# Half-precision products for the second experts' down projection, and GpSimd's stores without a turn marker

## The chip, the core and the metric

The kernel runs on one core of a Trainium2 chip. Its time is the device time of one execution in microseconds; smaller is better. The core's engines run their own instruction streams and wait for each other on semaphores: PE (TensorE, with PEld for its weight loads), DVE (VectorE), ACT (ScalarE), POOL (GpSimd) and SP (SyncE, which here only issues DMAs).

## The reference, cut to what matters

Two transformer layers of a gated cross-attention kind act on 64 x 64 tokens of width 128. Each layer adds an attention output and then the output of a mixture of eight experts, of which every token uses two. The last step, the one that the change touches most, is the second layer's mixture:

```python
perm = xf[rev]                               # 8192 slots, sorted by expert
chunks = perm.reshape(e, n * k // e, d)      # 8 experts x 1024 slots x 128
h = jax.nn.gelu(jnp.einsum('ecd,edf->ecf', chunks, w1), approximate=False)   # up, 128 -> 512
y = jnp.einsum('ecf,efd->ecd', h, w2).reshape(n * k, d)                      # down, 512 -> 128
y = y * sw[:, None]
out = jnp.zeros((n, d), dtype=x.dtype).at[rev].add(y)
```

The first layer's mixture has the same shape with relu and biases. All of it is in float32.

## The kernel before, in words

The work runs in four stages: first attention (0 to some 195 us of the trace), first experts (to 351), second attention (to 590), second experts (to the end). Each engine's order is written out by hand; the changes are in the two expert stages.

In an expert stage the 8192 slots are cut into tiles of 256: 32 tiles in four rounds of eight for the second experts; the first experts have four more tiles that serve two experts each. Rounds 2 and 3 are one loop body run twice, in a loop of the engine; rounds 1 and 4 are written out. Tile q goes through these steps:

- SP loads the tile's rows, gathered in DRAM, into `xin` (second experts: GpSimd gathers the first six tiles with indirect DMAs, line 592, and seven patches that SP stores back before it loads tile 6, lines 599 and 789).
- `gather` (PE, line 984): four half-precision transposes into PSUM; `parts` (DVE, line 1753) copies them to `xgT`.
- `up` (PE, line 996): twelve matmuls with 256 columns, in three half-precision products (high x high, high x low, low x high parts of the two factors).
- ACT's `step` (line 1281): gelu of 1024 columns from PSUM into `hid`, in float32.
- `down` (PE, line 1008): eight float32 matmuls with 128 columns, which the trace shows as sixteen rows.
- `result` (DVE, line 1777): two multiplications by the slots' weights into `yrow`.
- GpSimd's `step`: line 553, a multiplication of one element whose only use is its semaphore `turn`, and line 555, two indirect DMAs that store `yrow`. DVE waits for `turn` (line 1761) before it writes a `yrow` again.

PE's order in step q is gather of tile q+1, up of tile q, down of tile q-1. The expert of a tile is known only at run time. So for each `up` and each `down` PE's sequencer, the part of the engine that reads its instructions and hands the matmuls on, loads the expert's number (`expert`, line 1015) and computes weight addresses in its registers. These register instructions carry the line of the matmul that needs them, 803, since all matmuls go through `mm`.

Before the second experts, GpSimd scatters the tokens into DRAM (line 544) and SP loads `w2` after the last attention product (line 784).

Of the kernel before, what the change touches and what calls it, by code (L numbers as in the profile page):

```python
# [11 lines left out]
ALU = mybir.AluOpType  # L12
# [9 lines left out]
P = 128  # L22
# [48 lines left out]
def build(nc, A, out):  # L71

    ctx = ExitStack()
    with ctx:
# [69 lines left out]
        turn = sb("turn", [1, XS_LEAD])  # L144
# [29 lines left out]
        w2 = sb("w2", [P, E * FF])  # L174

# [56 lines left out]
        yrow = at(18.5, [XS_LEAD, 2, D])  # L232
        yc = at(44, [4, CT_TILES, TOPK, D])
# [29 lines left out]
        def banks(b, n):  # L263
# [31 lines left out]
        w2_in = sem("w2_in")  # L295
# [4 lines left out]
              (("xin", XS_LEAD), ("xT", 2), ("xT_sb", 2), ("up", 2), ("hid", 2), ("y", 2), ("yrow", 2), ("turn", 1),  # L300
# [13 lines left out]

        def turns(l, i, q):
            if l == 1 and isinstance(i, int) and i == 0:
                return (ROUNDS - (q >= MIXED)) * XS_LEAD + q + 1
            return l * TILES[0] + (i - 1) * XS_LEAD + q + 1
# [162 lines left out]
        def _(pool):  # L481
# [66 lines left out]
            def experts(l):  # L548

                def step(i, q):  # L550
                    pool.wait_ge(ff["yrow"][q % 2], i * (XS_LEAD // 2) + q // 2 + halves(l) + 1)

                    g.tensor_tensor(turn[:, q:q + 1], lane[0:1, :], lane[0:1, :], ALU.mult).then_inc(ff["turn"][0], 1)  # L553
                    for u in range(2):
                        g.indirect_dma_start(  # L555
                            ys[l], bass.IndirectOffsetOnAxis(xin[:, q, u, :].bitcast(U32)[:, D:D + 1], 0),
                            yrow[:, q, u, :], None).then_inc(ff["stored"][q], 16)

                expert_tiles(pool, l, step)
# [77 lines left out]
        def _(sp):  # L637
# [161 lines left out]
        def _(pe):  # L799
# [162 lines left out]
            def experts(l):  # L962
                f, m0 = ff, halves(l)
                pe.wait_ge(w1_lo[l], E)
                if l == 1:
                    pe.wait_ge(w2_in, 16)
# [33 lines left out]
                def down(i, q, es):  # L1000
                    v, m = q % 2, i * (XS_LEAD // 2) + q // 2 + m0
                    pe.wait_ge(f["hid"][v], m + 1)
# [13 lines left out]

                def round_(i, n, last):

                    first = isinstance(i, int) and i == 0
                    for q in range(n):  # L1020
                        late = first and (q == 0 or l == 1 and q == HEAD0 - 1)
                        if q < n - 1:
                            if not late:
                                gather(i, q + 1)
                        elif not last:
                            gather(i + 1, 0)
                        up(i, q, expert(i, q))
                        if q >= 1:
                            down(i, q - 1, expert(i, q - 1))
                        elif not first:  # L1030
                            down(i - 1, XS_LEAD - 1, expert(i - 1, XS_LEAD - 1))
                        if late:
                            gather(i, q + 1)
# [6 lines left out]
                if l == 0:  # L1040
                    pe.wait_ge(left, 1)
                    round_(ROUNDS, MIXED, True)
                    down(ROUNDS, MIXED - 1, expert(ROUNDS, MIXED - 1))
                else:
                    down(ROUNDS - 1, XS_LEAD - 1, expert(ROUNDS - 1, XS_LEAD - 1))
# [151 lines left out]
        def _(act):  # L1197
# [58 lines left out]
            def experts(l):  # L1256
# [6 lines left out]
                def step(i, q):  # L1263
                    v, m = q % 2, i * (XS_LEAD // 2) + q // 2 + m0
                    act.wait_ge(f["up"][v], m + 1)
                    wait(act, f["y"][v], m)
# [47 lines left out]
            for g in range(G0, G1):  # L1314
# [47 lines left out]
                for c in route_at("copy", g):  # L1362
                    route_copy(1, c)
            experts(1)
# [6 lines left out]
        def _(dve):  # L1371
# [374 lines left out]
            def experts(l):  # L1746
# [9 lines left out]
                def result(i, q):  # L1756
# [3 lines left out]
                    if l == 1 or not (isinstance(i, int) and i == 0):  # L1760
                        dve.wait_ge(f["turn"][0], turns(l, i, q))
# [13 lines left out]
                    for u in range(2):  # L1775
                        w = xin[:, q, u, :].bitcast(F32)[:, D + 1:D + 2]
                        ins = v_.tensor_scalar(yrow[:, q, u, :], y[:, u, :], w, None, ALU.mult)  # L1777
                    ins.then_inc(f["yrow"][v], 1)

                def round_(i, n, last):  # L1780
                    first = isinstance(i, int) and i == 0
                    for q in range(n):
# [4 lines left out]
                        if q >= 1:  # L1787
                            result(i, q - 1)
                        elif not first:
                            result(i - 1, XS_LEAD - 1)  # L1790
# [10 lines left out]
                else:  # L1801
                    result(ROUNDS - 1, XS_LEAD - 1)
# [95 lines left out]
            route_table(1)  # L1898
            experts(1)
# [50 lines left out]
```

## Time and profile before

| | us |
|---|---|
| median of three runs | 751.6 (748.81 to 752.73) |
| the profiled execution | 751.48 |
| its span, first to last instruction | 749.9 |
| PE busy | 543.9 (73%) |
| DVE busy | 416.3 (56%) |
| POOL busy | 330.3 (44%) |
| ACT busy | 231.4 (31%) |

What lies outside the span is 1.6 us. Busy shares are means over four stages with different limits, so the rows below are taken from the stages that the change touches.

### The profile page before, as it was taken

How to read it: one execution, taken by the hardware profiler on the slowest of the kernel's cores; microseconds unless marked ns; L12 is line 12 of the kernel's file. 1: busy time of each engine (PE TensorE's matmuls, PEld its weight loads, DVE VectorE, ACT ScalarE, POOL GpSimd, SP SyncE). 2: the span in 40 equal slices, each digit the busy share in tenths (PEclk: the TensorE clock that was granted, in tenths of full speed). 3: DMA queues.
4: the chain of work that ended last, by engine and by line, in shares of the span. 5: the costliest groups of instructions: out<-in, count | busy, mean ns of one | idle time of the engine just before them, and what ended most of it. 6: DMA issues, size and time to landing. Idle time of an engine off the chain costs nothing.

```text
span 749.9 us, 16972 instructions
## 1 busy us (share of the span) xinstructions
PE 543.9 (73%) x5388; PEld 427.4 (57%) x5389; DVE 416.3 (56%) x1474; ACT 231.4 (31%) x411; POOL 330.3 (44%) x412
## 2 busy tenths in 40 slices
PE   1687958515699999962798888696871487999950
PEld 1355646402289999952354567575650175989950
DVE  4785496997523333314896378878678421223315
ACT  0321011123044444432621365454542031323210
POOL 6202005777536666634500000071657676656650
PEclk9878685855799999996689999888665599999985
DMA  7911001123222222411763255453333123322219
GB/s 206 264 46 35 23 14 34 50 96 100 72 76 83 73 77 79 122 65 52 242 200 125 69 153 163 112 133 81 68 100 104 45 55 105 80 79 77 72 51 321
DMA packets 70254, 74.97 MB, mean 100 GB/s; under 512 B 12216, under 2 KB 58552, under 8 KB 70120
## 3 DMA queue, kind: packets, MB, share of 16 engines
q1 hardware_dynamic: 55240, 49.64, 24.1%
q0 software_dynamic: 9968, 21.88, 9.4%
q10 hardware_dynamic: 4976, 2.53, 1.2%
q8 instruction: 43, 0.70, 0.4%
q14 instruction: 27, 0.22, 0.1%
HBM read 45.62 MB, written 28.29 MB: 99 GB/s over the span
## 4 chain that ended last, share of the span: by engine, by line
PE 54%; DVE 20%; issue 8%; POOL 8%; DMA 6%; ACT 2%; SPq 1%; POOLq 0%; DVEq 0%; ACTq 0%
PE PS L803 49%; POOL xs L544 5%; DMA work<-ys 3%; DVE XN L1424 2%; PE PS L984 2%; DVE X L1381 2%; DVE work L1381 1%; DVE work L1865 1%; POOL work L592 1%; DVE rtmp L1381 1%; DVE stats L1386 1%; PE PS L1145 1%; POOL work L599 1%; PE PS L832 1%; DVE nwt L1381 1%
## 5 line engine op out<-in xcount | busy, mean ns | idle before, releaser
L544 POOL DMA_INDIRECT xs<-pack,adr_i x80 | 78.0, 975 | 188.8 <-ACT pack L1220 136.5
L555 POOL DMA_INDIRECT ys<-work x136 | 132.6, 975 | 33.2 <-issue 33.2
L803 PE MATMUL PS<-w,work 128*128 x1088 | 134.8, 277 | 7.2 <-issue 7.1
L803 PEld LDWEIGHTS PS<-w,work 128*128 128x128 f32 x1088 | 126.7, 192 | 12.5 <-issue 11.2
L803 PE MATMUL PS<-work,w1h 128*128 128x256 f16 (+1 forms) x576 | 97.5, 271 | 3.1 <-issue 1.6
L1381 DVE TENSOR_TENSOR work<-PS,work 128x128 f32<-128x128 f32 (+3 forms) x82 | 31.9, 391 | 94.2 <-PE PS L803 50.3
L803 PE MATMUL PS<-work 97*64 97x256 f16 (+5 forms) x608 | 73.6, 309 | 13.9 <-DVE work L1530 7.6
L803 PE MATMUL PS<-work,w1l 128*128 128x256 f16 (+1 forms) x288 | 77.7, 270 | 0.0
L1278 ACT ACTIVATE work<-PS,b 128x256 f32<-128x256 f32 x128 | 50.3, 475 | 77.5 <-PE PS L803 77.5
L803 PE MATMUL PS<-ones 128*128 128x512 f16 x195 | 53.6, 437 | 25.6 <-DVE rows_i L1660 12.4
L803 PEld LDWEIGHTS PS<-work 97*64 97x64 f16 (+2 forms) x608 | 56.7, 162 | 24.6 <-DVE work L1530 10.8
L1777 DVE TENSOR_SCALAR work<-PS,work 128x128 f32<-128x128 f32 x64 | 19.5, 346 | 78.2 <-PE PS L803 78.2
L1281 ACT ACTIVATE work<-PS 128x1024 f32<-128x1024 f32 x32 | 32.8, 1024 | 84.0 <-PE PS L803 84.0
L803 PEld LDWEIGHTS PS<-work,w1h 128*128 x576 | 51.4, 99 | 11.6 <-issue 4.9
L544 POOL DMA_INDIRECT xs<-work,adr_i x48 | 47.3, 986 | 15.3 <-issue 12.8
L1865 DVE TENSOR_REDUCE work<-PS 128x16 f32<-128x1024 f32 x32 | 39.1, 1222 | 25.8 <-PE PS L803 25.8
L803 PEld LDWEIGHTS PS<-ones 128*128 128x128 f16 x195 | 20.7, 111 | 55.5 <-issue 41.0
L803 PE MATMUL PS<-work,W 128*128 128x512 f32 x60 | 45.7, 884 | 8.5 <-DVE work L1381 2.8
L553 POOL TENSOR_TENSOR turn<-lane 1x1 f32<-1x1 f32 x68 | 16.4, 241 | 75.3 <-DVE work L1777 75.1
L1753 DVE COPY work<-PS 128x512 f16<-128x512 f16 x68 | 28.3, 417 | 32.6 <-PE PS L984 32.5
L1320 ACT ACTIVATE XN<-PS,mask_bias 128x1024 f32<-128x1024 f32 x32 | 35.6, 1114 | 20.2 <-PE PS L803 19.3
L803 PE MATMUL PS<-ident,work 128*64 128x36 f32 x512 | 25.1, 249 | 17.0 <-DVE work L1381 17.0
(290 smaller groups left out, 856.4 us busy)
## 6 DMA issues: line engine op xcount, KB each, us to landing
work<-ys SPq DMA_DIRECT2D x12, 512.0 KB, 6.0
work<-xs SPq DMA_DIRECT2D x32, 130.0 KB, 2.3
work<-xs SPq DMA_DIRECT2D x60, 65.0 KB, 1.9
k_parts<-work SPq DMA_DIRECT2D x24, 128.0 KB, 2.0
w<-k_parts SPq DMA_DIRECT2D x8, 384.0 KB
work<-k_parts SPq DMA_DIRECT2D x32, 96.0 KB
work<-q_parts SPq DMA_DIRECT2D x8, 384.0 KB
work<-q_parts SPq DMA_DIRECT2D x32, 96.0 KB
```

What stands on the lines that cost most here:

```text
L544: g.indirect_dma_start(xs[l], bass.IndirectOffsetOnAxis(adr_i[:, k, T:T + 1], 0), pack_of(l, c)[:, s, k, :].bitcast(U32), None)\
L553: g.tensor_tensor(turn[:, q:q + 1], lane[0:1, :], lane[0:1, :], ALU.mult).then_inc(ff["turn"][0], 1)
L555: g.indirect_dma_start(ys[l], bass.IndirectOffsetOnAxis(xin[:, q, u, :].bitcast(U32)[:, D:D + 1], 0), yrow[:, q, u, :], None).then_inc(ff[ ...
L803: return t.matmul(o, lhsT, rhs, start=start, stop=stop, skip_group_check=True)
L984: ins = t.transpose(o[:, h, u, :], xin[:, q, u, h * D:(h + 1) * D], ident16[:])
L1278: ins = a.activation(hid[:, v, c, :], PF[:, b * 512 + c * TILE:b * 512 + (c + 1) * TILE], ACT.Relu, bias=b1[:, ds(e * FC + c, 1)], scale=1 ...
L1281: ins = a.activation(hid[:, v, :, :].rearrange("p c n -> p (c n)"), banks(b, 1024), ACT.Gelu, scale=1 / WSCALE)
L1320: a.activation(pexp[:, T % 2, :], banks(2, 1024), ACT.Exp, bias=mask_bias[:, T:T + 1]).then_inc(p_done, 1)
L1381: return v_.tensor_tensor(o, x, y, op)
L1753: v_.tensor_copy(xgT[:, v, :, :].rearrange("p h n -> p (h n)"), PS[:, v, 0:TILE].bitcast(F16))\
L1777: ins = v_.tensor_scalar(yrow[:, q, u, :], y[:, u, :], w, None, ALU.mult)
L1865: v_.tensor_reduce(rmaxq[:, c % 2, s, :], banks(0, 1024).rearrange("p (h k) -> p h k", h=H), AX, ALU.max).then_inc(s_max, 1)
```

## The change

The second experts' down projection multiplies half-precision parts, as the up projection does. ACT applies gelu twice, once in float32 into `hid` and once in half precision into `hid_hi`; DVE subtracts (`low`) and leaves the rest in `hid_lo`. `w2` is loaded to another place, `w2raw`, as soon as the last scores are computed; ACT makes its high part `w2h`, DVE its low part `w2l`, each in one instruction of 4096 columns. A tile's down projection becomes 24 half-precision matmuls with 128 columns, and it runs two tiles behind the up projection instead of one. In both expert stages GpSimd's `turn` marker and DVE's wait for it go, and GpSimd's loop is written out.

```diff
             def experts(l):
-                def step(i, q):
+                for tile in range(TILES[l]):
+                    i, q = divmod(tile, XS_LEAD)
                     pool.wait_ge(ff["yrow"][q % 2], i * (XS_LEAD // 2) + q // 2 + halves(l) + 1)
-                    g.tensor_tensor(turn[:, q:q + 1], lane[0:1, :], lane[0:1, :], ALU.mult).then_inc(ff["turn"][0], 1)
                     for u in range(2):
                         g.indirect_dma_start(
...
-            sp.wait_ge(st_ps, NT)
-            sp.wait_ge(w1_lo[1], E)
-            sp.dma_start(w2[:].rearrange("p (e c d) -> p e c d", e=E, c=FC),
+            sp.wait_ge(s_ps, NT)
+            sp.dma_start(w2raw.rearrange("p (e c d) -> p e c d", e=E, c=FC),
...
+                    if l == 1:
+                        if isinstance(i, int) and i == 0 and q == 0:
+                            pe.wait_ge(w2_split, 2)
+                        pe.wait_ge(hid_low, i * XS_LEAD + q + 1)
...
+                    if l == 1:
+                        for u in range(2):
+                            for c in range(FC):
+                                w = ds(es[0] * FF + c * D, D)
+                                hi, lo = (h[:, q % 4, c, u * P:(u + 1) * P] for h in (hid_hi, hid_lo))
+                                for k, (h, w_) in enumerate(((hi, w2h), (hi, w2l), (lo, w2h))):
+                                    ins = mm(PS[:, 6 + v, u * D:(u + 1) * D], h, w_[:, w],
+                                             start=c == 0 and k == 0, stop=c == FC - 1 and k == 2)
+                        ins.then_inc(f["y"][v], 1)
+                        return
...
+                behind = l + 1
...
-                        if q >= 1:
-                            down(i, q - 1, expert(i, q - 1))
+                        if q >= behind:
+                            down(i, q - behind, expert(i, q - behind))
...
-                        ins = a.activation(hid[:, v, :, :].rearrange("p c n -> p (c n)"), banks(b, 1024),
-                                           ACT.Gelu, scale=1 / WSCALE)
+                        for h in (hid[:, v, :, :], hid_hi[:, q % 4, :, :]):
+                            ins = a.activation(h.rearrange("p c n -> p (c n)"), banks(b, 1024), ACT.Gelu, scale=1 / WSCALE)
...
+            a.activation(w2h, w2raw, ACT.Copy, scale=WSCALE).then_inc(w2_split, 1)
             experts(1)
...
-                        dve.wait_ge(f["turn"][0], turns(l, i, q))
...
+                def low(i, q):
+                    v, m = q % 2, i * (XS_LEAD // 2) + q // 2 + m0
+                    dve.wait_ge(f["hid"][v], m + 1)
+                    dve.wait_ge(f["y"][v], m - 1)
+                    flat = [h.rearrange("p c n -> p (c n)") for h in
+                            (hid_lo[:, q % 4, :, :], hid[:, v, :, :], hid_hi[:, q % 4, :, :])]
+                    tt(*flat, ALU.subtract).then_inc(hid_low, 1)
...
             route_table(1)
+            dve.wait_ge(w2_split, 1)
+            v_.scalar_tensor_tensor(out=w2l, in0=w2raw, scalar=WSCALE, in1=w2h,
+                                    op0=ALU.mult, op1=ALU.subtract).then_inc(w2_split, 1)
             experts(1)
```

```order
L1015 TENSOR_LOAD eidx_i
L1015 ISA x2
L803 ISA
L803 MATMUL PS<-w,work 128x128
L803 ISA
L803 MATMUL PS<-w,work 128x128
L803 ISA
L803 MATMUL PS<-w,work 128x128
L803 ISA
L803 MATMUL PS<-w,work 128x128 x5
L984 MATMUL PS<-ident,work 128x128 x4
```

Now, with the middle left out, in which an ISA with one matmul and an ISA with two take turns:

```order
L1022 TENSOR_LOAD eidx_i
L1022 ISA x2
L797 ISA
L797 MATMUL PS<-w,work 128x128
L797 ISA
L797 MATMUL PS<-w,work 128x128 x2
L797 ISA
...
L797 ISA
L797 MATMUL PS<-w,work 128x128 x14
L976 MATMUL PS<-ident,work 128x128 x4
```

A down projection had four address instructions and eight matmuls; it has eight and 24.

On DVE, from the end of the routing table to the first results of the second experts, before (COPY is `parts`, TENSOR_SCALAR `result`):

```order
L1660 CAST rows_i<-row_f 128x64
L1753 COPY work<-PS 128x512 x3
L1777 TENSOR_SCALAR work<-PS,work 128x128 x2
L1753 COPY work<-PS 128x512
L1777 TENSOR_SCALAR work<-PS,work 128x128 x2
```

And now, where the SCALAR_TENSOR_TENSOR makes `w2l` and the TENSOR_TENSOR is `low`:

```order
L1680 CAST rows_i<-row_f 128x64
L1936 SCALAR_TENSOR_TENSOR w<-work,w 128x4096
L1773 COPY work<-PS 128x512 x3
L1401 TENSOR_TENSOR work<-work 128x1024
L1773 COPY work<-PS 128x512
L1401 TENSOR_TENSOR work<-work 128x1024
L1799 TENSOR_SCALAR work<-PS,work 128x128 x2
```

The 4096-column instruction stands ahead of the stage's first copy, and a subtraction of 1024 columns comes in between the copy and the results of each tile.

On GpSimd, at the end of the first experts and the start of the additions behind them, before:

```order
L553 TENSOR_TENSOR turn<-lane 1x1
L555 DMA ys<-work 12288x128 x2
L553 TENSOR_TENSOR turn<-lane 1x1
L555 DMA ys<-work 12288x128 x2
L578 TENSOR_TENSOR work<-work 128x4x128 x2
L578 TENSOR_TENSOR w1h<-w1h 128x4x128 x2
```

And now, all 72 stores of the first experts in one row:

```order
L542 DMA xs<-pack,adr_i 36864x130 x16
L542 DMA xs<-work,adr_i 36864x130 x16
L552 DMA ys<-work 12288x128 x72
L573 TENSOR_TENSOR work<-work 128x4x128 x2
L573 TENSOR_TENSOR w1h<-w1h 128x4x128 x2
```

Nothing stands between the stores any more.

## Rows read from the trace of the kernel before

**Rows 1.** Chain of waits, three places (start us, us, work)
```profile
344.70 4.14 POOL turn L553
...
592.76 2.28 DMA xs<-pack,adr_i
595.90 1.01 POOL work L592
...
616.08 3.08 DMA work<-xs,fixadr_i
619.22 4.34 DMA xs<-work
625.70 1.90 DMA work<-xs
628.50 4.41 PE PS L803 x28
```

**Rows 2.** Timeline of TensorE, one tile of the last round (start us, us)
```profile
701.52 0.38 PE L803 MATMUL PS<-work,w1h 128*128 128x256 f16 x2
...
702.83 1.95 PE L803 MATMUL PS<-w,work 128*128 x16
704.62 0.39 PE L984 MATMUL PS<-ident,work 128*128 128x128 f16 x4
704.84 0.38 PE L803 MATMUL PS<-work,w1h 128*128 128x256 f16 x2
```

**Rows 3.** Line 1015 on TensorE's sequencer: loop pass 1, pass 2, last round
```profile
L1015 PEldq TENSOR_LOAD <-eidx_i x16: 297/302/417, 638.2 to 664.2; - x16
...
L1015 PEldq TENSOR_LOAD <-eidx_i x17: 297/301/350, 666.4 to 693.5; - x17
...
L1015 PEldq TENSOR_LOAD <-eidx_i x13: 299/302/310, 696.7 to 716.2; - x13
```

**Rows 4.** Line 803 on TensorE's sequencer, 331.5 to 332.5 us
```profile
L803 PEldq FUSED_REGOPS  x8: 46/46/51, 331.5 to 332.4; - x8
```

**Rows 5.** Timeline of TensorE, the same tile
```profile
331.65 2.05 PE L803 MATMUL PS<-w,work 128*128 x16 [1.33 <-issue]
```

**Rows 6.** Busy time by stretch (us, then PE, PEld, DVE, ACT, POOL busy; PEclk)
```profile
331.00:337.00 6.00, 4.16 (x40) 3.34 (x40) 1.07 (x4) 2.28 (x9) 2.50 (x4) 1.00 0.08 25
```

**Rows 7.** Timeline of VectorE, 157 us
```profile
157.45 0.68 DVE L1381 TENSOR_TENSOR pack<-XN,pack 128x512 f16<-128x512 f32 x1
```

**Rows 8.** Timeline of GpSimd, 157 us
```profile
157.79 1.19 POOL L544 DMA_INDIRECT xs<-work,adr_i  x1 [0.30 <-issue]
```

**Rows 9.** Timeline of VectorE, 197 us
```profile
197.84 3.47 DVE L1816 MEMSET work<- 128x4096 uint32 x1 [0.79 <-issue]
```

**Rows 10.** Timeline of GpSimd, 199 us
```profile
199.11 0.97 POOL L544 DMA_INDIRECT xs<-work,adr_i  x1 [0.30 <-issue]
```

**Rows 11.** Timeline of VectorE, 590 to 601 us
```profile
590.54 0.19 DVE L1660 CAST rows_i<-row_f 128x64 int32<-128x64 f32 x1
600.22 0.42 DVE L1753 COPY work<-PS 128x512 f16<-128x512 f16 x1 [9.49 <-PE PS L984]
```

**Rows 12.** Timeline of GpSimd, 591 us
```profile
591.49 0.96 POOL L544 DMA_INDIRECT xs<-pack,adr_i  x1 [0.30 <-issue]
```

**Rows 13.** Page, costliest groups: ACT, DVE (busy us, mean ns, idle before)
```profile
L1777 DVE TENSOR_SCALAR work<-PS,work 128x128 f32<-128x128 f32 x64 | 19.5, 346 | 78.2 <-PE PS L803 78.2
L1281 ACT ACTIVATE work<-PS 128x1024 f32<-128x1024 f32 x32 | 32.8, 1024 | 84.0 <-PE PS L803 84.0
...
L1865 DVE TENSOR_REDUCE work<-PS 128x16 f32<-128x1024 f32 x32 | 39.1, 1222 | 25.8 <-PE PS L803 25.8
```

**Rows 14.** Timeline of TensorE, last tile
```profile
717.90 0.38 PE L803 MATMUL PS<-work,w1h 128*128 128x256 f16 x2
```

**Rows 15.** Timeline of GpSimd, last tile's stores
```profile
724.87 0.98 POOL L555 DMA_INDIRECT ys<-work  x1 [0.16 <-issue]
726.16 0.97 POOL L555 DMA_INDIRECT ys<-work  x1 [0.30 <-issue]
```

More of the change, by code:

```diff
@@ L143, in build @@
         pack = sb("pack", [P, 2, CT_TILES, TOPK, ROW16], F16)
-        turn = sb("turn", [1, XS_LEAD])
         zrow = sb("zrow", [P, ROW16], F16)
@@ L174, in build @@
         w2 = sb("w2", [P, E * FF])
+        w2h, w2l = (w2[:, u * E * FF // 2:(u + 1) * E * FF // 2].bitcast(F16) for u in range(2))
         WORK = int(109.5 * 1024)
@@ L232, in build @@
         yrow = at(18.5, [XS_LEAD, 2, D])
+        hid_hi = at(28, [4, FC, TILE], F16)
+        hid_lo = at(36, [4, FC, TILE], F16)
+        w2raw = at(77.5, [E * FF])
         yc = at(44, [4, CT_TILES, TOPK, D])
@@ L299, in build @@
         ff = {k: [sem(f"f_{k}{u}") for u in range(n)] for k, n in
-              (("xin", XS_LEAD), ("xT", 2), ("xT_sb", 2), ("up", 2), ("hid", 2), ("y", 2), ("yrow", 2), ("turn", 1),
+              (("xin", XS_LEAD), ("xT", 2), ("xT_sb", 2), ("up", 2), ("hid", 2), ("y", 2), ("yrow", 2),
                ("stored", XS_LEAD), ("biased", 1))}
@@ L313, in rows_in @@
             return (ROUNDS * 16 + (q < MIXED) * 32) + i * 32
[L315 to L318, printed above, removed]
         y_sum = sem("y_sum")
@@ L1027, in round_ @@
                         up(i, q, expert(i, q))
-                        if q >= 1:
-                            down(i, q - 1, expert(i, q - 1))
+                        if q >= behind:
+                            down(i, q - behind, expert(i, q - behind))
                         elif not first:
-                            down(i - 1, XS_LEAD - 1, expert(i - 1, XS_LEAD - 1))
+                            j = XS_LEAD + q - behind
+                            down(i - 1, j, expert(i - 1, j))
                         if late:
@@ L1044, in experts @@
                 else:
-                    down(ROUNDS - 1, XS_LEAD - 1, expert(ROUNDS - 1, XS_LEAD - 1))
+                    for j in range(XS_LEAD - behind, XS_LEAD):
+                        down(ROUNDS - 1, j, expert(ROUNDS - 1, j))
             experts(0)
@@ L1265, in step @@
                     act.wait_ge(f["up"][v], m + 1)
-                    wait(act, f["y"][v], m)
+                    if l == 0:
+                        wait(act, f["y"][v], m)
+                    else:
+                        act.wait_ge(f["y"][v], m - 1)
+                        if q >= 2 or not isinstance(i, int) or i > 0:
+                            act.wait_ge(hid_low, i * XS_LEAD + q - 1)
                     b = 2 + 2 * v
@@ L1363, in _ @@
                     route_copy(1, c)
+            act.wait_ge(w2_in, 16)
+            act.wait_ge(st_ps, NT)
+            act.wait_ge(w1_lo[1], E)
+            a.activation(w2h, w2raw, ACT.Copy, scale=WSCALE).then_inc(w2_split, 1)
             experts(1)
@@ L1776, in result, with before @@
                         w = xin[:, q, u, :].bitcast(F32)[:, D + 1:D + 2]
-                        ins = v_.tensor_scalar(yrow[:, q, u, :], y[:, u, :], w, None, ALU.mult)
+                        if l == 0:
+                            ins = v_.tensor_scalar(yrow[:, q, u, :], y[:, u, :], w, None, ALU.mult)
+                        else:
+                            ins = v_.tensor_scalar(yrow[:, q, u, :], y[:, u, :], w, 1 / WSCALE, ALU.mult, ALU.mult)
                     ins.then_inc(f["yrow"][v], 1)
+                def low(i, q):
[5 more added lines that the diff above has]
+                    tt(*flat, ALU.subtract).then_inc(hid_low, 1)
+                def before(step, i, q, back):
+                    if q >= back:
+                        step(i, q - back)
+                    elif not (isinstance(i, int) and i == 0):
+                        step(i - 1, XS_LEAD + q - back)
                 def round_(i, n, last):
-                    first = isinstance(i, int) and i == 0
                     for q in range(n):
@@ L1786, in round_ @@
                             parts(i + 1, 0)
[L1787 to L1790, printed above, removed]
+                        if l == 1:
+                            before(low, i, q, 1)
+                        before(result, i, q, l + 1)
                 parts(0, 0)
@@ L1801, in experts @@
                 else:
+                    low(ROUNDS - 1, XS_LEAD - 1)
+                    result(ROUNDS - 1, XS_LEAD - 2)
                     result(ROUNDS - 1, XS_LEAD - 1)
```

8 lines of the change are left out of this document (3 added, 5 removed).

## The prediction

> **What bounds the kernel now.** I read the chain of waits first. It shows which of the changed places the end hangs on [rows 1]. At the end of the first experts it is GpSimd's turn marker at 344.70 us, which takes 4.14 us for one element. Ahead of the second experts it is GpSimd's scatter, then its gathers from 595.90 on; the last patch gather at 616.08, its transfer, SP's store of the patches at 619.22 and SP's load at 625.70 release tile 6, and from 628.50 on it is matmuls alone.
>
> Then I read the timeline of TensorE over one tile of the last round [rows 2]. The up projection starts at 701.52, the down projection at 702.83, the transposes at 704.62 and the next up at 704.84: 1.31 + 1.79 + 0.22 = 3.32 us, without a gap.
>
> Third comes what the busy time leaves out, TensorE's sequencer. The expert's number is loaded twice per tile, so the starts of these loads give its pace [rows 3]. From 638.2 to 666.4 (the first load of the second pass) eight tiles take 28.2 us, 3.53 each; the second pass takes 27.1, 3.39 each; the last round from 696.7 to 716.2 six tiles in 19.5, 3.25 each. In the first pass that is more than the array's 3.32. So two limits lie side by side, the array and the instruction stream in front of it, and the change moves them in opposite directions.
>
> What one address instruction costs is read where a tile of two experts needs eight in a row: 331.5 to 332.4 us, seven steps in 0.9 us, 0.13 each though each is counted as 46 ns [rows 4]. The window's ends are rounded; I take 0.125. There TensorE waited 1.33 us for issue alone [rows 5]: its sequencer does bound it when a tile needs more instructions.
>
> **Second experts, steady part.** On the array a down projection goes from sixteen rows to 24 half-precision matmuls of 128 columns. Four transposes of that shape and the step to the next up take 0.22 us [rows 2], 0.055 each with the weight load hidden, so 24 x 0.055 = 1.32 instead of 1.79 us. The array's tile falls to 2.85 us. On the sequencer, the order shows eight address instructions per down instead of four: 4 x 0.125 = +0.50 us per tile, and in the loop one more register instruction on average, some +0.1 (40 instead of 32 in eight tiles). That makes 3.75 in the written rounds (3.25 + 0.50), 4.13 in the first pass, 3.99 in the second. The sequencer wins everywhere.
>
> From up of tile 5 (628.50 [rows 1]) to up of tile 31 (717.90 [rows 14]) the trace takes 89.4 us for 26 tiles. Now: 3 x 3.75 + 8 x 4.13 + 8 x 3.99 + 7 x 3.75 = 102.5, **+13.1**. The ends of this term: if the sequencer's steps were free, 26 x 2.85 + 1.1 for the slower first tile (4.41 against 3.32 [rows 1]) = 75.2, -14.2; if each address instruction costs the 0.14 that rounding leaves room for, +14.7. I take the sequencer's value, since it is the nearest row to what is added.
>
> The other engines stay below 3.75. ACT does two activations of 1.02 us; DVE a copy of 0.42, two products of 0.35 and a subtraction, whose nearest row is 1.22 us for 1024 columns: 2.3 us [rows 11, 13]. The down projection's new wait for `low` looks two tiles back, and nothing but TensorE's own queue stands behind it. DVE's wait for ACT has the result and the next copy queued behind it, needed a tile later; ACT's wait is for a subtraction of two tiles ago. GpSimd's two stores are 1.29 apart, 2.6 us per tile [rows 15]. SP's earlier load of `w2` and ACT's split, about four times 1.02 us, lie ahead of the stage, beside the 10 us in which DVE has nothing to do before the first copy [rows 11]: nothing.
>
> **The end.** From the start of the last up to the end of the last store the trace takes 9.2 us (717.90 to 727.13 [rows 14, 15]). Three down projections now follow that up instead of two. The first ends after half a tile of sequencing, 1.7, eight address steps, 0.9, and fourteen matmuls, 0.8: 3.4. Result and hand-over 0.8, the last subtraction in the way up to 1, then three tiles of stores, 7.4. Together 12.6: **+3.4**. Without that subtraction +2.4; if stores were spaced by down projections alone, not below +1.
>
> **Turn marker.** It goes in 68 tiles, but only the last of the first experts stands in the chain: **-4.1** [rows 1]. It stood still while DVE cleared a mask; the store takes its place in GpSimd's queue. The same clearing at 197.84, 3.47 us [rows 9], has a GpSimd indirect DMA from 199.11 inside it, which took 0.97 [rows 10]: the store is not held. So the gain stays, between 0 and -4.1. The Trainium skill, page "SBUF — State Buffer", section "SBUF: two separate sides", warns that GpSimd cannot write its descriptors during a DVE instruction of the two-port kind; by it the store would wait in the marker's place and this term would be 0. The trace speaks against that for this instruction, 0.97 us.
>
> **Splitting w2 on DVE.** The new instruction of 4096 columns reads two SBUF tensors, and GpSimd still scatters beside it. How such a pair behaves is shown at 157 us: DVE's subtraction of two SBUF tensors runs from 157.45 for 0.68 us [rows 7], an indirect DMA begins at 157.79 and takes 1.19 instead of 0.97 [rows 8]; it waits for the subtraction's end, less about 0.13. The length: 512 columns 0.68, 1024 columns 1.22 [rows 13], so 4096 about 0.68 + 7 x 0.54 = 4.5 us, from 590.7 [rows 11] to 595.2. The scatter of 591.49 [rows 12] would stand till 595.1 and end at 595.9 rather than 592.5. One more scatter and the whole chain to tile 6 come behind it: **+3.5**, between 0 and 3.7.
>
> **Subtractions beside the gathers.** From 595.90 to 616.08 GpSimd issues a gather every 1.26 us [rows 1]. The subtractions of the first four tiles (1.2 us each, two SBUF inputs) fall among them, and each meets one gather's start. Held between 0 and 1.1 us, 0.45 on average, times four: **+1.8**, between 0 and 4.4.
>
> **Sum** on the profiled execution (751.48, its span 749.9, 1.6 outside; the median of the runs is 751.6): -4.1 + 3.5 + 1.8 + 13.1 + 3.4 = +17.7, so **769 us**.
>
> **The rivals.**
>
> *The array bounds, the sequencer does not* (0.10). For it: in the second pass and the last round the loads come at 3.39 and 3.25, so near to 3.32 that a full queue could be what paces them. Then a down projection saves 0.47 us, and the sum is -14.2 + 3.4 + 3.5 + 1.8 - 4.1 = -9.6: 742 us, faster. It decides as soon as four more address instructions cost less than the queue has in reserve. Against it: the first pass at 3.53, and 1.33 us of issue in rows 5. The Trainium skill ("TensorE: Matmul & The Clock Gate", section "Back-to-back issue gap") gives some 81 ns for a load-and-multiply pair of 128 columns in a real kernel; by that figure, an estimate, 24 take 1.94 us and this rival ends near 758. The trace has 55 ns.
>
> *GpSimd is not held by DVE* (0.12). The two holds go: 769 - 5.3 = 764 us. For it: GpSimd ran at 0.97 inside the clearing; against it: rows 7 and 8 show the very kind of instruction that is added.
>
> *The store stands still where the marker stood* (0.06), by the rule named with the marker: 773 us. Rows 9 and 10 speak against it.
>
> *The clock falls* (0.02). TensorE would be busy for 2.85 of 3.75 us, and an array at 1.2 instead of 2.4 GHz would need twice 2.85 us per tile: about 820 us. Against it: busy 4.16 of 6.00 us, it kept 1.00 [rows 6].
>
> **Chances.** The forecast has 0.65, the rivals 0.30, and 0.05 is left for a sequencer term near half its size and a change of next to nothing. The range, 757 to 776, reaches from half the sequencer's term with the holds cut to a third up to the lost marker with dearer holds; it leaves out the array rival and the clock. Within 0.5% (747.8 to 755.4 here, about what a measurement can tell from no change) 0.06, faster 0.09, slower 0.85.
>
> **What would show it.** Right: expert loads some 3.7 to 4.1 us apart per tile, eight address instructions in each down, TensorE idle for issue between up and down, matmul starts in `down` first 0.12 per pair and then 0.055; no marker and stores at 344.8; the second-last scatter at about 4.5 us; tile 6 released some 1 us later than now (at -4.1 + 5.3). Wrong: tiles at 2.85 to 3.3 us without issue gaps, or GpSimd's scatters unchanged at 0.97 beside the split. The forecast falls with the first of these; the second moves it by 5 us.

## The result

The changed kernel takes 772.3 us in the median (771.8 to 773.4, four runs), the kernel before 750.2 beside it on the same chip (747.0 to 752.7). The ratio is 1.032, with a 95% interval from 1.027 to 1.038: slower by 22 us. The profiled execution took 773.35, its span is 771.6.

Parts of the program that no edit touched vary by several us from trace to trace, and they go with TensorE's granted clock: from GpSimd's first addition behind the first experts to its first scatter of the second routing, the twelve traces of this study read 128.5 to 128.9 us where the clock of that stretch was 0.90, and 136.2 to 136.4 where it was 0.84. So small terms are read from stages with fixed ends, and whole times only where they differ by more.

In the rows of the changed kernel L797 is every matmul, L976 the transposes, L1022 the load of the expert's number, L1401 the subtraction, L552 GpSimd's stores, L542 its scatters, L587 and L594 its gathers. PEldq is TensorE's sequencer.

**Second experts.** The sequencer's loads of the expert's number, which answer to [rows 3], in the first loop pass, the second and the last round (count, shortest/median/longest in ns, first and last start in us):

```profile
L1022 PEldq TENSOR_LOAD <-eidx_i x16: 297/304/448, 644.6 to 676.0; - x16
...
L1022 PEldq TENSOR_LOAD <-eidx_i x16: 298/302/483, 678.1 to 708.4; - x16
...
L1022 PEldq TENSOR_LOAD <-eidx_i x16: 297/302/397, 710.3 to 738.8; - x16
```

From first load to first load a pass takes 33.5 and 32.2 us, 4.19 and 4.02 per tile instead of 3.53 and 3.39. The rows of one down projection, as in [rows 4]:

```profile
L797 PE MATMUL PS<-w,work x15: 219/227/228, 715.0 to 716.2; 128*128 x15
L797 PEldq FUSED_REGOPS  x8: 46/46/46, 714.9 to 715.8; - x8
```

Eight address instructions (FUSED_REGOPS) between 714.9 and 715.8, and the matmuls strung out behind them. The timeline of TensorE over a tile of the last round, as in [rows 2]:

```profile
728.51 0.39 PE L797 MATMUL PS<-work,w1h 128*128 128x256 f16 x2
...
730.27 1.87 PE L797 MATMUL PS<-w,work 128*128 x24 [0.28 <-issue]
731.99 0.39 PE L976 MATMUL PS<-ident,work 128*128 128x128 f16 x4
732.33 0.39 PE L797 MATMUL PS<-work,w1h 128*128 128x256 f16 x2
```

The tile takes 3.82 us, and 24 half-precision matmuls take 1.72, hardly less than the 1.79 of the eight in single precision. In the page's costliest groups, which take both expert stages together, the down projection stands with 12.3 us of idle time for issue, 7.1 before:

```profile
L797 PE MATMUL PS<-w,work 128*128 x1344 | 131.3, 246 | 16.9 <-issue 12.3
```

From the up of tile 5 to the up of tile 31 it is 103.9 us now, 89.4 before. The granted clock of this stretch is 1.00, that is 2.4 GHz, but for tile 5 of the kernel before: it took 4.47 us at a mean of 0.74, part of it at 1.2 GHz, and takes 3.37 at 1.00 now.

**GpSimd beside DVE.** The end of the first experts, GpSimd's timeline and then DVE's:

```profile
342.75 4.91 POOL L552 DMA_INDIRECT ys<-work  x1 [0.37 <-DVE work L1797]
347.97 0.96 POOL L552 DMA_INDIRECT ys<-work  x1 [0.30 <-issue]
```

```profile
343.28 3.47 DVE L1855 MEMSET work<- 128x4096 uint32 x1 [0.80 <-issue]
```

No marker is left, but the store stands where it stood, to 0.91 us behind the clearing's end. The marker [rows 1] had begun 0.56 us ahead of its clearing, the store begins 0.53 ahead:

```profile
345.26 3.47 DVE L1819 MEMSET work<- 128x4096 uint32 x1 [0.65 <-issue]
```

Ahead of the second experts, DVE and then GpSimd:

```profile
588.41 4.42 DVE L1936 SCALAR_TENSOR_TENSOR w<-work,w 128x4096 f16<-128x4096 f32 x1
...
608.26 1.22 DVE L1401 TENSOR_TENSOR work<-work 128x1024 f16<-128x1024 f32 x1 [1.34 <-ACT work L1298]
...
610.43 1.23 DVE L1401 TENSOR_TENSOR work<-work 128x1024 f16<-128x1024 f32 x1 [0.61 <-ACT work L1298]
...
613.98 1.22 DVE L1401 TENSOR_TENSOR work<-work 128x1024 f16<-128x1024 f32 x1
```

```profile
589.25 4.41 POOL L542 DMA_INDIRECT xs<-pack,adr_i  x1 [0.30 <-issue]
...
608.49 1.82 POOL L587 DMA_INDIRECT work<-xs,headadr_i  x1 [0.30 <-issue]
610.62 1.87 POOL L594 DMA_INDIRECT work<-xs,fixadr_i  x1 [0.30 <-issue]
612.79 0.95 POOL L594 DMA_INDIRECT work<-xs,fixadr_i  x1 [0.30 <-issue]
614.04 1.98 POOL L594 DMA_INDIRECT work<-xs,fixadr_i  x1 [0.30 <-issue]
```

Each long GpSimd row begins inside a DVE row with two SBUF inputs and ends 0.83 behind it: the scatter [rows 12] 4.41 instead of 0.96, three gathers 1.8 to 2.0 instead of 0.95.

**The end.** The last up begins at 735.93, the last store ends at 748.64:

```profile
740.59 1.70 POOL L552 DMA_INDIRECT ys<-work  x1 [0.77 <-DVE work L1799]
...
747.68 0.96 POOL L552 DMA_INDIRECT ys<-work  x1 [0.30 <-issue]
```

That is 12.7 us; before it was 9.2 [rows 14, 15].

### The profile page after: what moved, and what is told of

It is laid out like the page before. It is cut to its first block, busy times and chain, and to the rows that moved or that the text cites. A ratio compares the mean times of both kernels' runs of the same rounds, so it can differ in the third digit from the quotient of the medians.

```text
span 771.6 us, 17610 instructions
## 1 busy us (share of the span) xinstructions
PE 545.0 (71%) x5644; PEld 413.2 (54%) x5645; DVE 456.9 (59%) x1507; ACT 264.0 (34%) x444; POOL 348.6 (45%) x344
## 4 chain that ended last, share of the span: by engine, by line
PE 47%; DVE 26%; issue 10%; POOL 9%; DMA 5%; ACT 1%; SPq 1%; DVEq 0%; POOLq 0%
PE PS L797 43%; POOL xs L542 5%; DVE work L1401 3%; DVE XN L1444 3%; DMA work<-ys 3%; DVE X L1401 2%; DVE stats L1406 2%; PE PS L976 2%; POOL work L587 1%; DVE work L1901 1%; POOL ys L552 1%; DVE rtmp L1401 1%; POOL work L594 1%; DVE nwt L1401 1%; PE PS L1156 1%
## 5 line engine op out<-in xcount | busy, mean ns | idle before, releaser
L552 POOL DMA_INDIRECT ys<-work x136 | 161.2, 1186 | 113.7 <-DVE work L1797 65.1
L542 POOL DMA_INDIRECT xs<-pack,adr_i x80 | 81.4, 1017 | 189.8 <-ACT pack L1231 136.2
L797 PE MATMUL PS<-w,work 128*128 x1344 | 131.3, 246 | 16.9 <-issue 12.3
L797 PEld LDWEIGHTS PS<-w,work 128*128 128x128 f16 (+1 forms) x1344 | 115.3, 138 | 34.3 <-issue 27.2
L797 PE MATMUL PS<-work,w1h 128*128 128x256 f16 (+1 forms) x576 | 97.8, 271 | 6.4 <-issue 4.0
L1401 DVE TENSOR_TENSOR work<-PS,work 128x128 f32<-128x128 f32 (+3 forms) x82 | 31.9, 392 | 94.2 <-PE PS L797 74.8
L1298 ACT ACTIVATE work<-PS 128x1024 f32<-128x1024 f32 x64 | 62.0, 1021 | 71.2 <-PE PS L797 71.1
L797 PE MATMUL PS<-work 97*64 97x256 f16 (+5 forms) x608 | 70.9, 305 | 13.8 <-DVE work L1550 7.5
L797 PE MATMUL PS<-work,w1l 128*128 128x256 f16 (+1 forms) x288 | 77.8, 270 | 0.0
L797 PE MATMUL PS<-ones 128*128 128x512 f16 x195 | 54.0, 438 | 25.3 <-DVE rows_i L1680 12.4
L797 PEld LDWEIGHTS PS<-work 97*64 97x64 f16 (+2 forms) x608 | 54.5, 158 | 24.2 <-DVE work L1550 10.8
L797 PEld LDWEIGHTS PS<-work,w1h 128*128 x576 | 49.8, 99 | 19.1 <-issue 11.3
L542 POOL DMA_INDIRECT xs<-work,adr_i x48 | 47.3, 986 | 15.3 <-issue 12.8
L797 PE MATMUL PS<-work,W 128*128 128x512 f32 x60 | 44.2, 858 | 8.5 <-DVE work L1401 2.8
L797 PEld LDWEIGHTS PS<-ones 128*128 128x128 f16 x195 | 20.6, 111 | 55.0 <-issue 40.2
L1401 DVE TENSOR_TENSOR work<-work 128x1024 f16<-128x1024 f32 (+2 forms) x48 | 47.3, 985 | 2.5 <-ACT work L1298 2.0
L797 PE MATMUL PS<-ident,work 128*64 128x36 f32 x512 | 25.8, 253 | 19.8 <-DVE work L1401 19.8
```

The lines of the kernel that those rows point to most:

```text
L542: g.indirect_dma_start(xs[l], bass.IndirectOffsetOnAxis(adr_i[:, k, T:T + 1], 0), pack_of(l, c)[:, s, k, :].bitcast(U32), None)\
L552: g.indirect_dma_start(ys[l], bass.IndirectOffsetOnAxis(xin[:, q, u, :].bitcast(U32)[:, D:D + 1], 0), yrow[:, q, u, :], None).then_inc(ff[ ...
L797: return t.matmul(o, lhsT, rhs, start=start, stop=stop, skip_group_check=True)
L1298: ins = a.activation(h.rearrange("p c n -> p (c n)"), banks(b, 1024), ACT.Gelu, scale=1 / WSCALE)
L1401: return v_.tensor_tensor(o, x, y, op)
```

## The experiments

**1. TensorE's second experts without address instructions.** The matmuls stay; numbers replace registers, and the loop is written out. With the address instructions the loads of the expert's number go too. That is possible because only in the first experts does the expert of a tile depend on the data: for the second the reference cuts the 8192 sorted slots into eight equal chunks, and the kernel fills `eidx_i` with the constants q // 4, so both kernels load and multiply numbers that were known when they were written.

```diff
+                    if l == 1:
+                        return ((i * XS_LEAD + q) // (TILES[1] // E),)
                     return (pe.value_load(eidx_i[0:1, l, ds(i * XS_LEAD + q, 1)], min_val=0, max_val=E - 1),)
...
+                if l == 1:
+                    for i in range(1, ROUNDS - 1):
+                        round_(i, XS_LEAD, False)
+                else:
+                    with pe.Fori(1, ROUNDS - 1) as i:
```

> The changed kernel, with the second experts of TensorE written out and the expert numbers as constants: no load of the expert's number and no address instruction is left on TensorE's sequencer in that stage; all matmuls, waits and other engines as they are. Theory (the sequencer sets the tile): the tile falls from 3.8-4.2 us to between 2.85 (the array) and 3.3 (GpSimd's two stores, 1.5 us each while a subtraction holds one); 26 tiles give -16 to -29 us, the kernel comes to 744-755 us from 772, and TensorE's idle time for issue goes. Rival 1 (the array sets it: a pair of load and multiply costs more than 55 ns among 24 in a row): no change, 770-774. Rival 2 (DVE's subtraction sets it, which the view of waits names as TensorE's releaser ahead of each down projection): no change either, and that wait grows to about 1 us per tile.

Measured: 740.4 us (738.6 to 742.5), ratio to the kernel before 0.988 (0.980 to 0.997): 32 us faster than the change, more than I expected (744 to 755), and about 1% faster than before it. TensorE over a tile, and the busy time in 32 us of the steady part (PE, PEld, DVE, ACT, POOL, then PEclk):

```profile
685.30 0.38 PE L797 MATMUL PS<-work,w1h 128*128 128x256 f16 x2
...
686.61 1.50 PE L797 MATMUL PS<-w,work 128*128 128x128 f16 x24
687.95 0.39 PE L976 MATMUL PS<-ident,work 128*128 128x128 f16 x4
688.17 0.38 PE L797 MATMUL PS<-work,w1h 128*128 128x256 f16 x2
```

```profile
640.00:672.00 32.00, 31.93 (x446) 30.29 (x445) 23.12 (x45) 21.32 (x22) 25.00 (x22) 1.00 0.33 90
```

The tile is 2.87 us, the array's 2.85 within rounding, and TensorE is busy throughout. From up 5 to up 31 it is 76.3 us instead of 103.9. Both rivals fall: 24 matmuls take 1.34 us, 56 ns each, and the wait for DVE's subtraction is gone. How much of the 27.6 us is loads and how much addresses, this run does not split; experiment 2 prices the addresses. In the changed kernel the wait for DVE stands in the view of waits (680 to 709 us: total, times, longest), and it is a lesson in reading it:

```profile
PE PS L797 <- DVE work L1401: 1.4, 4, 0.4
```

The subtraction that ended last is named as releaser, though the down projection needs the one of a tile earlier, long done.

**2. Four address instructions more, in the kernel before.** The same price from the other side.

```diff
+                            off = c * D + (l == 1 and u == 1) * (D // 2 if c < FC - 1 else -D // 4)
                             ins = mm(PS[:, 6 + v, u * D:(u + 1) * D], hid[:, v, c, u * P:(u + 1) * P],
-                                     w2[:, ds(e * FF + c * D, D)], start=c == 0, stop=c == FC - 1)
+                                     w2[:, ds(e * FF + off, D)], start=c == 0, stop=c == FC - 1)
```

> The kernel before, single precision and one tile behind, with four more address instructions in each down projection of the second experts and nothing else added: the second half of a tile multiplies columns of w2 at an offset of its own, so its rows of the output are not the reference's. Theory (each address instruction costs TensorE's sequencer 0.125 us, whatever the matmuls are): tiles go from 3.53 / 3.39 / 3.25 of sequencer to 4.03 / 3.89 / 3.75, so from the up of tile 5 to the up of tile 31 about 101 us instead of 89.4, +10 to +12 on the whole. Rival (the added time in the changed kernel came from its 24 matmuls or from DVE's subtraction): 89-91 us for that stretch, no change of the whole.

Measured: 758.3 us, ratio 1.013 (1.007 to 1.018). From up 5 to up 31 it is 100.5 us (624.76 to 725.28) instead of 89.4, and the tiles of the two passes take 4.01 and 3.85 us each. A down projection on TensorE, now with idle time for issue:

```profile
700.99 2.05 PE L803 MATMUL PS<-w,work 128*128 x16 [0.29 <-issue]
```

Four instructions cost 11.1 us in 26 tiles. Without tile 5, whose clock differs (0.74 before, 1.00 here), it is 11.8 us in 25 tiles, 0.47 per tile beside the forecast's 0.50. Nothing of half precision, of DVE or of the distance is in it.

**3. The kernel before without address instructions**, the edit of 1.

> The kernel before, with TensorE's second experts written out and expert numbers as constants, as in after_fixed. Theory: what is left is the array's tile, 3.32 us; from the up of tile 5 to that of tile 31 26 x 3.32 + 1 = 87 us instead of 89.4, so -2 on the whole; after_fixed took 76.3 there, and the difference, 11 us, is what half precision gives once the sequencer is out of the way. Rival (most of after_fixed's gain is the writing out itself): that stretch falls by 10 us or more here too.

Measured: ratio 0.998 (0.994 to 1.002), no change that can be told. The stretch takes 86.1 us at a clock of 1.00, 3.32 for a tile of the loop. So in this stretch writing out alone gives 3.3 us, of which 1.1 is tile 5 and its clock (3.32 instead of 4.47); half precision gives 10 more on top of it (86.1 to 76.3), and without it costs 14.5.

**4. One tile behind instead of two**, on top of 1.

```diff
-                behind = l + 1
+                behind = 1
...
+                        if late:
+                            gather(i, q + 1)
                         if q >= behind:
```

> after_fixed with the down projection one tile behind the up projection instead of two (the late gather of the first round moved ahead of the down projection so that nothing deadlocks). Theory: after an up projection ACT needs 2.0 us for two gelus and DVE 1.2 for the subtraction, 3.5 with the hand-overs; one tile behind, TensorE has only 2.85 us of other work in that time, so the tile goes from 2.93 to 3.5-3.6: from up 5 to up 31 91-94 us instead of 76.3, the end about 1 us shorter, 753-757 on the whole. Rival (the distance does not matter, TensorE has enough queued): 740.

Measured: 756.3 us, ratio 1.009 (1.006 to 1.012), 16 us more than in experiment 1. In TensorE's waits from 650 to 690 us (total, times, longest):

```profile
PE PS L797 <- DVE work L1407: 3.9, 11, 0.4
```

Here the releaser is real: the tile is 3.39 us, 0.5 above the array's, and less than the 3.5 to 3.6 I expected (up 5 to up 31 88.2 instead of 91 to 94). The start of the stage lost as well: from the first gather to the up of tile 5 it is 37.4 us instead of 32.5, which I had not foreseen. The edit also moves a gather of the first round; whether that is the reason was not tested. That the whole time fell into the expected 753 to 757 is therefore luck. The distance of two is worth its buffers once the sequencer is out of the way.

**5. The kernel before without the turn marker.**

```diff
-                    g.tensor_tensor(turn[:, q:q + 1], lane[0:1, :], lane[0:1, :], ALU.mult).then_inc(ff["turn"][0], 1)
...
-                        dve.wait_ge(f["turn"][0], turns(l, i, q))
```

> The kernel before, with the turn marker alone taken out (GpSimd's stores of both experts written out without it, DVE waits for the stores alone). Theory, from the trace after the change (the store that stood behind the marker takes the marker's wait upon itself): the store beside the clearing of the mask takes about 4.9 us instead of marker 4.14 and store 0.97, the time stays at 749-751. Rival (my prediction's term: the marker costs 4.1): 746. A marker also costs some tenths per tile in the tail of both experts: at most -0.5.

Measured: 753.7 us, ratio 1.003 (0.998 to 1.007). GpSimd at the end of the first experts:

```profile
344.85 4.91 POOL L554 DMA_INDIRECT ys<-work  x1 [0.37 <-DVE work L1773]
350.07 0.97 POOL L554 DMA_INDIRECT ys<-work  x1 [0.30 <-issue]
```

From the second-last tile's first store to the last store's end 8.79 us instead of 8.91. The marker itself costs 0.1: the store takes its wait upon itself, as expected.

**6. The two long DVE instructions in eight pieces.**

```diff
-            v_.memset(kmask[:, 1, :, :, :], 0.0).then_inc(k_blank, 1)
+            for j in range(8):
+                ins = v_.memset(kmask[:, 1, j // 2, 2 * (j % 2):2 * (j % 2) + 2, :], 0.0)
+            ins.then_inc(k_blank, 1)
...
+            for e in range(E):
+                piece = slice(e * FF, (e + 1) * FF)
+                ins = v_.scalar_tensor_tensor(out=w2l[:, piece], in0=w2raw[:, piece], scalar=WSCALE, in1=w2h[:, piece],
+                                              op0=ALU.mult, op1=ALU.subtract)
+            ins.then_inc(w2_split, 1)
```

> The changed kernel, with two DVE instructions cut into eight pieces each: the clearing of the second mask at the end of the first experts (3.47 us), and the low half of w2 (4.42 us). Same work, same order. Theory (GpSimd stands still only until the end of the DVE instruction that runs when its transfer is issued): the store at 342.75 falls from 4.91 us to 1.0-1.5, the scatter at 589.25 from 4.41 to 1.0-1.6, two more GpSimd transfers may lose 0.5 each; together -4 to -7 us, 765-768. Rival (GpSimd stands still as long as DVE is at such work, in pieces or not): 771-773, and both transfers stay above 4 us.

Measured: 770.7 us, ratio 1.026 (1.019 to 1.033), against 1.032 (1.027 to 1.038) for the change. That is some 5 us less, but the intervals overlap, and the time is above the 765 to 768 I expected. The rows say more, GpSimd's and then DVE's:

```profile
348.00 0.97 POOL L552 DMA_INDIRECT ys<-work  x1 [0.37 <-DVE work L1797]
...
591.26 1.27 POOL L542 DMA_INDIRECT xs<-pack,adr_i  x1 [0.30 <-issue]
592.84 1.50 POOL L542 DMA_INDIRECT xs<-pack,adr_i  x1 [0.30 <-issue]
```

```profile
347.78 4.27 DVE L1856 MEMSET work<- 128x512 uint32 x8
```

The store is not held at all, and the end of the first experts is 3.9 us shorter (4.85 instead of 8.78 from the same two marks as in 5). The scatters lose 0.8 together instead of 3.4. So a held scatter waits for one instruction's end, not for DVE's work as a whole. The profiled execution hardly shows it as a whole, since in it GpSimd's first store of the first experts came at 220.2 instead of 214.6 us, ahead of all that was edited.

**7. The subtraction reads PSUM.** ACT writes the single-precision gelu back into its bank.

```diff
+                    if l == 1 and (q >= 2 or not isinstance(i, int) or i > 0):
+                        pe.wait_ge(hid_low, i * XS_LEAD + q - 1)
...
-                        for h in (hid[:, v, :, :], hid_hi[:, q % 4, :, :]):
-                            ins = a.activation(h.rearrange("p c n -> p (c n)"), banks(b, 1024), ACT.Gelu, scale=1 / WSCALE)
+                        a.activation(hid_hi[:, q % 4, :, :].rearrange("p c n -> p (c n)"), banks(b, 1024), ACT.Gelu,
+                                     scale=1 / WSCALE)
+                        ins = a.activation(banks(b, 1024), banks(b, 1024), ACT.Gelu, scale=1 / WSCALE)
...
+                    tt(lo, banks(2 + 2 * v, 1024), hi, ALU.subtract).then_inc(hid_low, 1)
```

> The changed kernel, with ACT writing the single-precision gelu back into its PSUM bank instead of SBUF, so that DVE's subtraction reads one operand from PSUM and one from SBUF; the up projection waits for the subtraction of two tiles ago instead of ACT alone. Theory (GpSimd stands still beside a DVE instruction with two SBUF inputs, not beside one that reads PSUM): the gathers at 608-614 fall from 1.8-2.0 us to 0.97, the stores of the last tiles from 1.70 to about 1.0; tile 6 is released 1.5 to 2.8 us earlier and the tail is 1 to 2 us shorter: 767-770; the tile itself stays at 3.8-4.2, since TensorE's sequencer sets it. Rival (DVE holds GpSimd whatever it reads): 772, gathers and stores as they were. Against both: ACT's write into PSUM or the new wait could lengthen the tile, 26 times 0.1 us.

Measured: 772.8 us, ratio 1.029 (1.022 to 1.036), again no different as a whole, where I had expected 767 to 770. The gathers of the stage's start, by line:

```profile
L587 POOL DMA_INDIRECT work<-xs,headadr_i x12: 952/955/997, 601.9 to 624.6; - x12
...
L594 POOL DMA_INDIRECT work<-xs,fixadr_i x7: 955/955/955, 614.5 to 622.1; - x7
```

None is held. From the first gather to the up of tile 5 it is 32.0 us instead of 34.9, and 12.0 instead of 12.7 at the end; the tile stays at 3.8 to 4.2. So the rival (DVE holds GpSimd whatever it reads) falls. What the profiled execution lacks went in the second attention, which the edit doesn't touch: from the end of the last store of the first experts to the first scatter it took 141.7 instead of 136.1 us. The granted clock (PEclk) differs there, 0.84 instead of 0.89; the busy times of the engines, as in experiment 1, for the change and then for this run, from GpSimd's first addition on:

```profile
354.48:485.03 130.55, 108.79 (x1406) 74.97 (x1406) 96.52 (x312) 57.31 (x85) 10.66 (x8) 0.89 0.52 151
```

```profile
356.21:492.42 136.21, 116.02 (x1410) 79.44 (x1414) 96.57 (x312) 57.91 (x85) 10.65 (x9) 0.84 0.48 145
```

**8. The clearing 0.8 us later**, behind five small DVE instructions (one profiled run).

```diff
-            v_.memset(kmask[:, 1, :, :, :], 0.0).then_inc(k_blank, 1)
             dve.wait_ge(w_late, 16 * NL)
...
             v_.tensor_scalar(wox[:], wox[:], gt[:, 1:2], None, ALU.mult)
+            v_.memset(kmask[:, 1, :, :, :], 0.0).then_inc(k_blank, 1)
```

> The changed kernel, with the clearing of the second mask moved behind the five small DVE instructions on the mask and the gate that follow it now (about 1.1 us in all). Theory, read from four traces (the clearing of 4096 columns has 0.8 us of idle DVE ahead of it, and the GpSimd instruction that begins in those 0.8 us stands still to the clearing's end, while those that began earlier or begin after the clearing has begun do not): the clearing starts about 1.1 us later; the store that took 4.91 takes 0.97, and the second store, which begins 1.27 us behind it, falls into the 0.8 us and takes 4 to 5 us in its place. Rival 1 (whatever GpSimd does in the 0.5 us before the clearing is what is held, by the distance alone): neither store is held, or the second only if it begins 0.5-0.6 us ahead. Rival 2 (the clearing holds any GpSimd instruction that overlaps it here): the first store stays at 4 to 5 us.

Measured: 772.0 us. GpSimd and DVE:

```profile
342.58 0.97 POOL L552 DMA_INDIRECT ys<-work  x1 [0.37 <-DVE work L1797]
343.86 0.97 POOL L552 DMA_INDIRECT ys<-work  x1 [0.30 <-issue]
```

```profile
344.09 3.47 DVE L1862 MEMSET work<- 128x4096 uint32 x1 [0.80 <-issue]
```

My theory falls: the second store begins inside DVE's 0.80 of idle time and is not held. The rival, that the distance alone decides, fits this run and falls by the rows of experiment 1, where a store that began 0.14 us behind the clearing's start stood to 0.90 behind its end (GpSimd, then DVE):

```profile
343.34 4.23 POOL L552 DMA_INDIRECT ys<-work  x1 [0.30 <-issue]
```

```profile
343.20 3.47 DVE L1861 MEMSET work<- 128x4096 uint32 x1 [0.80 <-issue]
```

So markers and stores that began from 0.57 ahead to 0.15 behind were held, in eight traces; here one that began 0.23 ahead was not, and at 197 us none was that began with the clearing or behind it. In the eight traces the clearing stands directly behind DVE's wait for `tails`; here and at 197 us other DVE instructions stand between a wait and the clearing. The first piece in experiment 6, also directly behind that wait, held nothing. Whether the place behind the wait is part of the condition no run tests, and the cause stays open. The cure is seen in this one trace: the end of the first experts is 3.9 us shorter, as with the pieces.

**9. All together, and all but PSUM.**

> All that helped together: the changed kernel with TensorE's second experts written out, the clearing and the low half of w2 in eight pieces each, and the subtraction reading PSUM. From after_fixed (740): -3.9 for the store beside the clearing, -2.6 for the scatter beside w2's split, -2.5 for the gathers, -0.7 at the end: 730-733, if the second attention begins as much earlier as the last store does; 734-736 if it does not. Rival: the new wait of the up projection for the subtraction of two tiles ago costs more than it gives at a tile of 2.93 us (DVE is two thirds busy): 740 or more.

Measured: 737.2 us (735.8 to 742.2), ratio to the kernel before 0.987 (0.984 to 0.990).

> The changed kernel, with TensorE's second experts written out and the two long DVE instructions in eight pieces, the subtraction reading SBUF as in the changed kernel. It is the best version without the PSUM operand. Theory (at a tile of 2.9 us the operand from PSUM gives 0.7-0.9 at the end and takes 1.0 in the steady part, as the stages of the two traces read): 735-739, the same as with it. Rival (the holds of the gathers cost as much here as in the changed kernel, 2.9): 739-741.

Measured: 739.7 us (735.7 to 741.9), ratio 0.990 (0.986 to 0.993). Both beat both kernels; between them and experiment 1 the runs don't decide. By stages, with PSUM the stretch from up 5 to up 31 takes 77.3 us, without it 74.8; the end takes 11.1 and 12.0, the start 32.3 and 33.0. The 2.5 us between them are no measure of PSUM: with it, tile 5 ran at a granted clock of 0.52, nearly all of it at 1.2 GHz, and took 5.32 us instead of 2.87 (busy times again):

```profile
622.56:627.88 5.32, 5.32 (x42) 4.57 (x41) 1.57 (x3) 1.94 (x2) 0.00 (x0) 0.52 0.21 52
```

In both the store beside the clearing is free and the scatters nearly so (3.3 and 2.6 us less than in experiment 1), but the ratios, 0.987 and 0.990 beside 0.988, show none of these 6 us. My 730 to 736 for the first was too low, and for the second 739.7 lies with the rival (739 to 741) rather than with my 735 to 739, though its range of runs covers both.

## Why the prediction came out

The forecast, 769, was right in its sign, near in its size (772.3) and right in its largest mechanism. One of its five terms failed, and the rival that said so, at 0.06, had 773.

**Second experts, steady part**, +13.1: measured +14.5. The tiles came out at 3.81, 4.19 and 4.02 where 3.75, 4.13 and 3.99 stood. Without tile 5 and its clock it is +15.6 in 25 tiles. Experiments 1 and 2 show the cause from both sides: 27.6 us go when no load and no address instruction is left, 11.1 come when four address instructions are added to the old kernel. The rival of the clock falls: it stayed at 1.00. The rival of the array had the right array, 2.85 against 2.87 measured, and the wrong bound. The figure of the Trainium skill named with it ("TensorE: Matmul & The Clock Gate", section "Back-to-back issue gap"), 81 ns for a load and multiply of 128 columns, does not hold here: experiment 1 has 56 ns, 24 times in a row, without a gap.

**Splitting w2 on DVE**, +3.5: measured 3.45 (4.41 - 0.96), as the row at 157 us had it. DVE had no idle time ahead of its row, so ACT's part of the split held nothing, as forecast.

**Subtractions beside the gathers**, +1.8: measured +2.3 to the up of tile 5 (34.9 - 32.6); three of them held a gather, by 0.9 to 1.0 each, not four by 0.45, so the near size is luck in part. The three other traces of the old order read 31.5 to 31.7 where this one has 32.6, so the term is good to 1 us. With experiment 7 the whole amount goes.

**The end**, +3.4: measured +3.5, where two errors nearly cancel: the first of the last six stores began 4.66 us after the last up, not 5.2, and the six took 8.05, not 7.4, since a subtraction held the first of them.

**Turn marker**, -4.1: measured -0.1. This is the step that failed: "the store is not held", argued from an indirect DMA that began 1.3 us inside the other clearing [rows 9, 10]. That one is indeed not held; the store, which began 0.53 us ahead of the clearing, was, for 4.91 us. The rival that the store stands still where the marker stood, at 0.06, came true, and experiment 5 shows it alone. I took the kind of DVE instruction for the condition and overlooked that marker and store had nearly the same place in time. The Trainium skill's rule ("SBUF — State Buffer", section "SBUF: two separate sides"), that GpSimd and certain DVE instructions exclude one another for a whole instruction, fits the scatter and the gathers, which began inside a DVE row with two SBUF inputs. The clearing has no such input, and no run shows that the rule covers it: this store was held for 4.91, while transfers ran at 0.97 inside the other clearing and in experiment 8.

The terms as measured sum to 14.5 + 3.45 + 2.3 + 3.5 - 0.1 = 23.6; the last store ends 21.5 us later than before. The 2.1 between lie in stages that the change doesn't touch: at GpSimd's first store of the first experts the later trace was already 2.2 us ahead. Without them the profiled execution would have taken some 775, near the top of my range; that 772 came out nearer to 769 is luck. (The range's lower end, by its own words, is 759, not 757: 769 - 6.6 - 3.5.)

## What to carry over

Before matmuls are cut into more and cheaper ones, count what their addresses cost on TensorE's sequencer: here 0.12 us each (0.47 for four), more than two of the matmuls, and a change that lost 22 us won about 9 (ratio 0.988) when the expert numbers were written as constants. So ask first whether a number that a kernel loads is known beforehand. A GpSimd transfer beside a long DVE instruction can stand still to that instruction's end: let the subtraction read PSUM, cut the long instruction, or try it at another place. And a wait that a marker shows does not go with the marker; ask what stands in its place at the same time.

## What the hardware showed unexpectedly

- The clearing of 4096 columns in one piece has 0.64 to 0.80 us of idle DVE ahead of it in every trace; in pieces of 512 columns it has 0.05, and the pieces end 4.27 us after they began, just 3.47 + 0.80. Cut, it costs DVE nothing. Perhaps the 0.8 is not idle time but the clearing's own first part; no run shows which.
- That clearing held the GpSimd instruction beside it in eight traces, whether it began 0.57 us ahead or 0.15 behind; the clearing at 197 us, beside which three transfers run, holds none [rows 9, 10]. The condition is open.
- A stage that no edit touched took 128.5 to 136.4 us, and the order of its times is the order of its granted clocks, 0.90 down to 0.84. A tile of the second experts that ran at 0.52 took 5.32 us instead of 2.87.
